# Row-half products for attention's maxima, wider transfers, and pipelined norm stages in a four-stage transformer kernel

## The reference

```python
x = x + _layernorm(_L0_attn_ref(_layernorm(x), ...))   # 16 heads of 16, rope, softmax over all 2048 keys
x = x + _layernorm(_L0_ffn_ref(_layernorm(x), ...))    # 16 experts, the best 2 of each token, and a shared one
x = x + _layernorm(_L1_attn_ref(_layernorm(x), ...))   # gated delta rule, 32 heads of 128
x = x + _layernorm(_L1_ffn_ref(_layernorm(x), ...))    # silu(g) * u with int32 weights less 128, times a scale per row
```

## Time and profile before

| | us |
|---|---|
| three runs, median (lowest to highest) | 4075.34 (4071.72 to 4076.6) |
| the profiled execution | 4075.91 |
| its span | 4073.8 |
| PE, DVE, ACT, POOL busy | 3594.1, 2864.2, 2399.3, 1900.5 |
| mean granted clock of PE | 0.936 |

### The profile page before, as it was taken

One profiled execution on the slowest core, in us unless ns is written; L12 is line 12 of the kernel. 1 busy time (PEld: TensorE's weight loads), 2 busy tenths in 40 slices (PEclk: granted clock), 3 DMA queues, 4 the chain that ended last, 5 costly groups with the idle time before them and its releaser, 6 DMA issues. The chain is left out here.

```text
span 4073.8 us, 70395 instructions
## 1 busy us (share of the span) xinstructions
PE 3594.1 (88%) x22926; PEld 2232.0 (55%) x22926; DVE 2864.2 (70%) x6763; ACT 2399.3 (59%) x6452; POOL 1900.5 (47%) x4587
## 2 busy tenths in 40 slices
PE   6599999998598149999999999999999999998396
PEld 3123333223355126777777777777777777777253
DVE  4588888870422447888888888888888888886513
ACT  1066666673123047777777777777777777775110
POOL 3100000000300328777777777777777777776000
PEclk8599999997699579999999999999999999999698
DMA  7700000000512111111111111111111111110000
GB/s 144 100 1 1 1 1 1 1 1 3 200 54 87 36 37 28 38 23 37 39 39 28 39 39 27 32 38 39 28 39 39 29 38 32 38 28 22 33 0 21
DMA packets 204017, 148.95 MB, mean 37 GB/s; under 512 B 148708, under 2 KB 185445, under 8 KB 200466
## 3 DMA queue, kind: packets, MB, share of 16 engines
q1 hardware_dynamic: 200594, 136.16, 13.5%
q0 software_dynamic: 3072, 8.39, 0.6%
HBM read 102.43 MB, written 41.68 MB: 35 GB/s over the span
## 5 line engine op out<-in xcount | busy, mean ns | idle before, releaser
L1785 POOL TENSOR_TENSOR dl_blocks_tmp<-dl_blocks_l,dl_blocks_x 128x60 f32<-128x60 f32 (+24 forms) x1984 | 714.1, 360 | 305.7 <-DMA dl_blocks_l<-lm_dram 169.7
L1790 POOL TENSOR_TENSOR dl_blocks_x<-dl_blocks_x,dl_blocks_tmp 128x60 f32<-128x60 f32 (+24 forms) x1984 | 702.3, 354 | 155.4
L633 DVE TENSOR_REDUCE part_max<-mx 128x1 f32<-128x512 f32 x1024 | 637.1, 685 | 81.3 <-PE mx L495 81.2
L569 ACT ACTIVATE normed_t<-sc 128x1024 f32<-128x1024 f32 x512 | 496.4, 1021 | 222.2 <-PE sc L506 221.9
L1942 DVE SCALAR_TENSOR_TENSOR dl_conv<-dl_raw,dl_weights,dl_conv 128x512 f32<-128x512 f32 x768 | 581.3, 784 | 27.8 <-ACT dl_conv L1713 23.4
L1484 PE MATMUL prep<-normed_t,dl_weights 128*128 128x512 f32 x1024 | 482.8, 595 | 19.5 <-DMA dl_weights<-in_w_delta 17.3
L495 PE MATMUL mx<-k_t,q_t 96*128 96x512 bf16 x1024 | 375.0, 401 | 30.6 <-PEq L183 21.8
L476 POOL COPY v_staged<-v 128x256 f32<-128x256 f32 x16 | 6.3, 400 | 704.7 <-PE o_ps L518 704.6
L506 PE MATMUL sc<-q_t,k_t 99*128 99x512 bf16 x1024 | 305.5, 381 | 0.6
L1643 ACT ACTIVATE dl_q_state<-rec_a,t_neg_decay 128x128 f32<-128x128 f32 x512 | 160.4, 366 | 239.4 <-DVE dl_r L1847 239.4
L1589 PE MATMUL gate_y_ps<-dl_weights,dl_gated_t 128*128 128x256 f32 x1024 | 272.5, 389 | 0.9 <-ACT dl_gated_t L1658 0.9
(11 more groups left out here) (276 smaller groups left out, 7835.0 us busy)
## 6 DMA issues: line engine op xcount, KB each, us to landing
dl_blocks_l<-lm_dram SPq DMA_DIRECT2D x256, 128.0 KB, 2.6
dl_weights<-in_w_delta SPq DMA_DIRECT2D x16, 1032.0 KB, 5.0
lm_dram<-dl_lm SPq DMA_DIRECT2D x256, 32.0 KB, 1.7
xs_dram<-dl_blocks_x SPq DMA_DIRECT2D x64, 128.0 KB, 2.4
dl_inverse_t<-xs_dram SPq DMA_DIRECT2D x256, 32.0 KB
qk_dram<-hd_parts SPq DMA_DIRECT2D x16, 384.0 KB, 3.5
q_t<-qk_dram SPq DMA_DIRECT2D x12, 512.0 KB, 17.5
k_t<-qk_dram SPq DMA_DIRECT2D x12, 512.0 KB, 18.3
```

What stands on the lines that cost most here:

```text
L569: act.activation(probs[:, e % 2, u * 2 * BQ:(u + 1) * 2 * BQ], flat(sc[u][:, :, :]), ACT.Exp, scale=float(DH) ** -0.5).then_inc(s["exp_don ...
L633: dve.reduce_max(part_max[:, t % NT, x[2]:x[2] + 1], bank_of(x)[:, :], AX.X).then_inc(s["ring_read"], 1)
L1785: pool.tensor_tensor(out, L[:, 0:i, i].unsqueeze(1).broadcast_to([P, NM - c0, i]), Xs[:, c0:NM, i:i + 1].broadcast_to([P, NM - c0, i]), AL ...
L1790: pool.tensor_tensor(Xs[:, c0:NM, 0:i], Xs[:, c0:NM, 0:i], out, ALU.add).then_inc(s["solve_step"], 1)
```

## The change

1. `head_phase`: qk_dram is laid out by head, part and row. Each part of a block is stored by a transfer of its own. A read-back takes every second head at a time, in transfers of two bands (32 partitions) and, for k, two of one band; even heads have their leading four bands in rows 0 to 63 and the other two in 64 to 95, odd heads the leading ones in rows 64 to 127 and the others in 32 to 63. The halves come in the order q, k, k, q. The ones are no longer SP's.
2. `attention_phase`: a product for the maxima takes the four leading bands only (64 rows). Two such products, of head h and head h + 1, which is eight steps behind, make a pair on the two halves of the rows, into a double bank; a step has two pairs, and DVE reduces a double bank at once. LAG is 28. Scores go into three single banks, with an exponential of 512 columns each. Odd heads' score products take 128 rows, of which 29 are zeroed by POOL; maxima go to rows 96 to 98 or 0 to 2. POOL sets zeros and ones before it copies v of the third head.
3. `attn_out_phase` replaces turn, projection and the norm before the experts: groups of four tiles pass through turn, projection, bias (DVE), statistics, root (POOL), scaling (ACT), add, second norm and turn. The expert weights' loads and the clearing of rows_dram are issued in it.
4. `tail_phase` replaces the norm before the feed-forward, the feed-forward and the last norm, in groups of four tiles (two at the end). g, u and d weights are waited for and dequantised one by one; a block's down products come after the first two rounds of the next block.

```diff
@@ head_phase
-    Q_ORDER = ((0, 0), (1, 0), (2, 0), (3, 1), (4, 1), (5, 2))
-    K_ORDER = ((0, 0), (3, 0), (5, 0), (1, 1), (4, 1), (2, 2))
+    BANDS = (((0, 2, slice(1, 3)), (32, 2, slice(1, 3)), (64, 2, slice(0, 2))),
+             ((0, 2, slice(0, 2)), (32, 1, slice(1, 2)), (48, 1, slice(0, 1)), (64, 2, slice(1, 3))))
-            return n // (2 * GROUPS), n // GROUPS % 2, n % GROUPS
+            return n // (2 * GROUPS), (0, 1, 1, 0)[n // GROUPS], n % GROUPS
+                for part in range(3):
+                    sp.dma_start(a["qk_dram"][side, u, :, part, :, BT * b:BT * b + BT],
+                                 parts[n % DEEP][:, part, :]).then_inc(parts_out[n % DEEP], 16)
...
-                for part, src in (Q_ORDER, K_ORDER)[side]:
-                    sp.dma_start(dst[DH * part:DH * part + DH, HALF * u:HALF * u + HALF, :],
-                                 a["qk_dram"][side, u, src, :, :].rearrange("(h d) t -> d h t", d=DH)
-                                 ).then_inc(heads_in[u], 16)
+                for odd in range(2):
+                    for row, band, chosen in BANDS[side]:
+                        at = (row + 64 * odd) % P if row < 64 else 64 - 32 * odd
+                        sp.dma_start((QT, KT)[side][at:at + DH * band, HALF * u + odd:HALF * u + HALF:2, :],
+                                     a["qk_dram"][side, u, odd::2, chosen, :, :].rearrange("h c d t -> (c d) h t")
+                                     ).then_inc(heads_in[u], 16)
@@ attention_phase
-    LAG = NT + 4
-    RING = 3
+    LAG = NT + HALF + 4
+    RING = 2
+    LEAD = SPLIT_ROWS - 2 * DH
-        mx = [c.ps(ctx, f"mx{i}", [P, 512]) for i in range(RING)]
-        sc = [c.ps(ctx, f"sc{i}", [P, 2, 512]) for i in range(2)]
+        mx = [c.ps(ctx, f"mx{i}", [P, 2, 512]) for i in range(RING)]
+        sc = [c.ps(ctx, f"sc{i}", [P, 512]) for i in range(3)]
+        def pair(t, v):
+            if t < HALF or t >= STEPS - HALF:
+                h, q = (0, t) if t < HALF else (HEADS - 1, t - STEPS + NT)
+                return [(h, q, 2 * v), (h, q, 2 * v + 1)]
+            h, j = divmod(t - HALF, NT)
+            b = 2 * (j % 2) + v
+            return sorted([(h, HALF + j // 2, b), (h + 1, j // 2, b)], key=lambda x: x[0] % 2)
...
+                for i, (h, q, b) in enumerate(pair(t, v)):
+                    at = 64 * (h % 2)
+                    last = pe.matmul(bank_of(x)[:, i, :], QT[at:at + LEAD, h, q * P:(q + 1) * P],
+                                     KT[at:at + LEAD, h, b * 512:(b + 1) * 512], start=True, stop=True)
+                last.then_inc(s["ring_filled"], 1)
...
                 if t < STEPS:
                     maximum(t, 0)
                 if 0 <= e < STEPS:
                     scores(e, 0)
+                    scores(e, 1)
                 if t < STEPS:
                     maximum(t, 1)
                 if 0 <= e < STEPS:
-                    scores(e, 1)
-                if t < STEPS:
-                    maximum(t, 2)
+                    scores(e, 2)
                 if 0 <= e - 1 < STEPS:
                     weigh(e - 1)
-                if t < STEPS:
-                    maximum(t, 3)
+                if 0 <= e < STEPS:
+                    scores(e, 3)
@@ attn_out_phase (new), PE and SP
+            turn(0, c.Y, 0)
+            for g in range(GROUPS):
+                if g + 1 < GROUPS:
+                    turn(g + 1, c.Y, 2 * g + 2)
+                project(g)
+            for g in range(GROUPS):
+                pe.wait_ge(scaled, was["scaled"] + scaled_no[1, g] + 1)
+                turn(g, rows, 2 * GROUPS + 2 * g)
...
+            sp.dma_start(W[:, :, :], a["out_w"]).then_inc(s["w_in"], 16)
+            for j in range(2):
+                sp.dma_start(bias[:, j, :], a["out_b"].broadcast_to([P, D])).then_inc(s["w_in"], 16)
+            moe.load_shared(sp)
+            sp.wait_ge(s["zero_set"], 1)
+            moe.clear_rows(sp)
+            moe.load_experts(sp)
@@ tail_phase (new), PE
+            turn(0)
+            for b in range(NB):
+                for m in range(FT):
+                    widen(b, m)
+                    if b and m == EARLY - 1:
+                        for q in range(TILES):
+                            narrow(b - 1, q)
+                if b + 1 < NB:
+                    turn(b + 1)
+            for q in range(TILES):
+                narrow(NB - 1, q)
```

More of the change, by code:

```diff
@@ new lines, in project @@
+            def project(g):
+                if g == 0:
+                    pe.wait_ge(s["w_in"], 48)
+                pe.wait_ge(copied, was["copied"] + 2 * g + 2)
+                for i in range(2 * g, 2 * g + 2):
+                    if i >= 4:
+                        pe.wait_ge(s["biased"], i - 3)
+                    for j in range(2):
+                        t = 2 * i + j
+                        for k in range(KD):
+                            last = pe.matmul(ps[i % 4][:, j, :], c.XT[:, k, t * P:(t + 1) * P], W[:, k, :],
+                                             start=(k == 0), stop=(k == KD - 1))
+                    last.then_inc(s["proj_done"], 1)
@@ new lines, in normalise @@
+            def normalise(r, g):
+                act.wait_ge(rstd_done, was["rstd_done"] + 3 * number[r, g] + 4)
+                if r == 0 and g >= 2:
+                    act.wait_ge(added, was["added"] + g - 1)
+                for t in range(TILES * g, TILES * g + TILES):
+                    src, out = (c.Y[:, t, :], normed[g % 2][:, t - TILES * g, :]) if r == 0 else (
+                        c.X[:, t, :], rows[:, t, :])
+                    last = act.activation(out, src, ACT.Identity, bias=shift[r][:, t:t + 1],
+                                          scale=rstd[r][:, t:t + 1])
+                last.then_inc(scaled, 1)
@@ new lines, in turn @@
+            def turn(g):
+                pe.wait_ge(scaled, was["scaled"] + number["input", g] + 1)
+                for i in range(2 * g, 2 * g + 2):
+                    if i >= 2:
+                        pe.wait_ge(copied, was["copied"] + i - 1)
+                    for j in range(2):
+                        for k in range(KD):
+                            last = pe.transpose(tp[i % 2][:, j, k, :],
+                                                normed["input"][g % 2][:, 2 * (i % 2) + j, k * P:(k + 1) * P],
+                                                c.ident[:, :])
+                    last.then_inc(turned, 1)
@@ new lines, in widen @@
+            def widen(b, m):
+                n = FT * b + m
+                if n == 0:
+                    pe.wait_ge(s["dequantised"], 2)
+                if m == 0:
+                    pe.wait_ge(copied, was["copied"] + 2 * b + 2)
+                if n >= 2:
+                    pe.wait_ge(s["hidden_done"], n - 1)
+                for weights, ps, done in ((wg, g_ps, "g_done"), (wu, u_ps, "u_done")):
+                    for k in range(KD):
+                        last = pe.matmul(ps[m % 2][:, :], weights[:, k, m * P:(m + 1) * P],
+                                         c.XT[:, k, b * B:(b + 1) * B], start=(k == 0), stop=(k == KD - 1))
+                    last.then_inc(s[done], 1)
@@ new lines, in _ @@
+            copy(0)
+            act.wait_ge(s["d_in"], 64)
+            for b in range(NB):
+                for m in range(FT):
+                    n = FT * b + m
+                    act.wait_ge(s["g_done"], n + 1)
+                    if n >= 2:
+                        act.wait_ge(s["hidden_done"], n - 1)
+                    act.activation(sg[m % 2][:, :], g_ps[m % 2][:, :], ACT.Silu, scale=scale[:, 0, m:m + 1]
+                                   ).then_inc(s["silu_done"], 1)
+                if b + 1 < NB:
+                    copy(b + 1)
@@ L2040, in program @@
                 rows = c.sb(moe, "moe_rows", [P, NT, D], F32)
-                norm_phase(c, "ln1", only is None, normed=rows)
-                moe_phase(c, rows, a)
+                inputs = MoeInputs(c, moe, a)
+                attn_out_phase(c, a, rows, inputs)
+                moe_phase(c, rows, a, inputs)
             if only == "moe":
```

576 lines of the change are left out of this document (398 added, 178 removed).

## The result

The changed kernel takes **3934.9 us** (median of four runs, 3933.3 to 3938.9) against 4076.0 for the kernel before: the ratio is 0.9657, with a 95% interval of 0.964 to 0.9674. 3949 was forecast. The profiled execution took 3934.1 us, its span is 3932.4.

What follows compares the result with a forecast made beforehand. PE was taken to bound attention's full part, DVE its lead-in. Terms -28 (read-back), +37 (attention), -58 (projection, norms), -2 (experts), -75 (tail) sum to -126 us: 3949 us as a median, range 3805 to 4050.

Steps and rivals of the forecast that it cites:

- its own bounds: Bounds in us: read-back +5 and -36, attention +5 and +92, projection with norms -45 and -68, tail -65 and -80.
- 2.8 to 3.3: Attention's full part: step forecast at 3.05 us; below 2.8 or above 3.3 the prediction counts as wrong.
- rival C: Attention's pairs: the two halves run one after the other, starts 0.43 us apart; +98 us, in all 4047; chance 0.12.
- rival B: Attention: changes of shape by rows cost nothing in bf16 (gap 0.01 us); step 2.5, in all 3824 us; chance 0.20.
- rival D: Attention's full part: PE's clock stays at 1.2 GHz, 3 us more a step, slower than before, up to 4640; chance 0.08.
- skew: Attention's pairs: second product taken to add 0.03 us to 0.218; bounds of the case: none and 0.06.
- 8 x 0.213: Attention's weighing: eight records one after the other would take 8 x 0.213 us, against 1.0 seen; used to infer side-by-side running.
- POOL was idle there [...], so nothing: Head and attention: moving K's ones from SP to some 32 POOL memsets costs nothing, POOL being 5.6 us busy in 695.
- -13 - 8 - 8 = -29: Head: faster transfers at 205 GB/s shorten the read-backs before the last issue, q by 13 us, k twice by 8.
- nothing except in the last block: Head: SP's 32 more stores and 4 more loads, 0.47 us each, lie in its waits; last block +1 us.

Runs made afterwards that it cites:

- the nine others: Nine other kernels of the study in which q comes back by 32 partitions: attention's first product at 140.6 to 143.0 us, against 159.9 in the kernel before.

## Why the prediction was right, and where it was off

The forecast of faster holds. Each of the four parts lies within its own bounds, and the step (2.82, with the per-head work 2.92) within 2.8 to 3.3; the terms inside the parts were not all right.

**Part 3** (-60, measured -59.2): the expert stage comes 51.8 us behind attention for 52. This is in part luck. The first projection begins 7.2 us into the stage (953.03 less 945.84) where the prediction had 4.1 (953.7 less 949.6), PE having waited 4.73 us for the bias; the last projection ends 33.5 us in for 35; and the chain behind it takes 18.3 us for 15.

**Part 4** (-75, measured -74.9): first product at 16.9 for 16.7, end 6.7 for 8; PE has 172.6 us from first to last product, where one less than the 172.5 of before was forecast.

**Part 2** (+37, measured +17.3). The mechanism was right: pairs side by side (rival C's 0.43 is seen only where both products sit on one half, 3.25 us a step), changes of shape not free (rival B's 0.01 against 0.10 to 0.15), clock at 2.4 GHz after 9 us (rival D). The sizes were off by 20 us. The step makes -30 of it: four new changes at 0.105, not 0.12, and no skew in a pair where 0.03 was put, give 2.82 a step for 2.94; with the per-head work that is 2.92 for 3.05, times 228. Against that the lead-in is 69.2 for 65.5 and the end 72.0 for 66. One row was misread on the way: the weighing's eight records one after the other are not 8 x 0.213 but 8 x 0.427, by the 0.213 of the 256-column records in the earlier trace rows; four of its products at once then give the 0.853, which speaks for side by side all the more. The lead-in's reductions do come every 1.13 us (12 in 13.65):

```profile
157.49 13.65 DVE L678 TENSOR_REDUCE part_max<-mx 128x2 f32<-128x1024 f32 x12
```

but PE waits 4.7 us at the first head's end, which was not in the sum. There DVE's three casts for the splitting take 1.23, 1.61 and 1.61 us, 3.9 us more than the 0.17 each that they take for every later head and took here before. Each ends when one of POOL's new memsets of Q and K rows ends (DVE, POOL, and DVE at the second head):

```profile
198.51 1.61 DVE L656 CAST max_parts<-neg_max 128x16 bf16<-128x16 f32 x1
...
198.29 1.79 POOL L507 MEMSET k_t<- 3x2048 bf16 x1
...
245.35 0.17 DVE L656 CAST max_parts<-neg_max 128x16 bf16<-128x16 f32 x1
```

The step of the prediction that this refutes is that of the memsets, "POOL was idle there [...], so nothing": POOL had been idle there, but its memsets hold up DVE. That DVE's casts wait for the memsets is read from these times; no run moves the memsets away. In the end part a step is 2.39, not 2.25: ACT needs 2.06 for four activations and waits 0.33 for the fourth score, behind the weighing. That wait the prediction had named, but counted at nothing.

```profile
881.44 2.06 ACT L612 ACTIVATE normed_t<-sc 128x512 f32<-128x512 f32 x4 [0.33 <-PE sc L549]
```

**Part 1** (-28, measured -21.1, and -17 to -19 in the nine others). The rate was right: 212 GB/s for 205 while q came. The Trainium skill, SBUF — State Buffer, section Door 1: The DMA port swizzle, gives 189 at 32 partitions and 104 at 16; the runs agree in kind, with 212 and 122. The step that failed is "-13 - 8 - 8 = -29", that each gap gets shorter by what the rates take off the transfer. The three gaps between the issues of read-backs, 37.2, 37.2 and 32.6 us before, fell by 9.7, 2.8 and 4.5, 17.0 in all. In them (the landing of the last transfer of each read-back, and SP's timeline):

| us | q | first k | second k | sum |
|---|---|---|---|---|
| issue to last landing | -12.2 | -5.3 | -7.6 | -25.1 |
| last landing to ACT's start (q, first k) or to the next read-back (second k) | +1.1 | +1.0 | +3.1 | +5.2 |
| ACT's start to the next read-back's issue | +1.4 | +1.4 | | +2.9 |
| gap | -9.7 | -2.8 | -4.5 | -17.0 |

So the transfers alone gave -25 for -29, k's first one 3 us less than put. The second row is the slower stores, 192 for 384 GB/s, a term that the prediction didn't have: behind the second k all nine queued ones, 1.2 MB, must land, which takes 6.0 us for 2.9. It takes 6.0 as well with 16-partition read-backs in the new layout, and 3.0 with three stores per block in the old one. The third row is SP, which issues the three stores of a group's last block every 0.6 us, ahead of the read-back; the prediction had put that at nothing except in the last block. A last term was not forecast either and hides a part of the miss: from the last read-back's issue to the first product are 3.3 us for 8.0, since SP's issuing is quicker (2.9 us for 4.7) and it has no transfer of the ones to wait for. The size of that is shown by every kernel with the new head (3.2 to 3.7 us with 6 transfers) against the two without (8.0 and 7.8); which of the two makes it is argued.

**Not forecast:** 3.5 us in the experts, the second norm and the delta rule. The latter two run the same code, and between the kernels of this study they differ by 5 us (2435.6 to 2441.3); I take it for spread.

The terms -21 + 17 - 59 - 1 - 2 - 75 are -141. In the total the misses cancel in part, which is luck: part 1 is off by +7 and part 2 by -20, and part 2's -20 is itself -30 in the step against +10 in the lead-in and the end.

## What to carry to other kernels

Products on different halves of PE's rows run side by side, but each change between half and full rows costs 0.10 to 0.11 us here, half of a 512-column bf16 product: count the changes before the products, and put what has one shape together. Then look at who feeds those products: put together they need their buffers together, and the engine that frees them must have no small work in between. When a layout is changed for the sake of reads, look at the rate of the writes too: here it fell to half. Work that is put on an idle engine can hold up another one beside it, as the memsets on POOL did DVE's casts. The large and sure gains of such a change were the dull ones: pipelining norms, loads and products of stages that ran one after the other, 134 of 141 us.

## What the runs showed of the hardware

- Two 64x512 bf16 products, on rows 0 to 63 and 64 to 127, take 0.22 us together at 2.4 GHz (0.32 less the change behind them; a second pair right behind adds 0.23), on one half 0.43. No skew between them can be seen.
- A change of shape costs 0.10 to 0.11 us between 64 rows and 99 or 128, about 0.11 into the 128*32 weighing and 0.15 out of it; by steps with four, five and six changes 0.10 on the mean. Before, 96-row and 99-row products followed one another at no cost.
- Read-backs into 32 partitions move 212 GB/s, into 16 partitions 111 to 122.
- Stores of 128 KB move 192 GB/s with the DMA share at 0.55 in the layout by head, 374 with 1.08 in the old layout.
- A DVE cast of 128x16 took 1.61 us instead of 0.17 where a POOL memset ran beside it, and ended with it.
- Three stores of 128 KB instead of one of 384 KB, in the old layout, change nothing (1.0002, 0.9992 to 1.0011).
